# Attention loop of a bottleneck block on TensorE: in odd steps, maximum and logits ahead of the value product of four steps back

## What is computed

```python
qkv = conv2d(x, qkv_w, 0).reshape(b, 3, HEADS, HD, hw)
q, k, v = (qkv[:, 0], qkv[:, 1], qkv[:, 2])
r = (rw + rh).reshape(1, HEADS, HD, hw)
logits = jnp.einsum('bhdi,bhdj->bhij', q, k + r) * HD ** (-0.5)
a = jax.nn.softmax(logits, axis=-1)
out = jnp.einsum('bhij,bhdj->bhdi', a, v)
```

## Time and profile before

| | us |
|---|---|
| median of 3 runs | 3366.75 (3364.51 to 3368.51) |
| the profiled execution | 3367.39 |
| its span on the core | 3365.7 |
| PE busy | 3077.0 |
| DVE busy | 1934.3 |
| ACT busy | 1616.3 |
| POOL busy | 873.6 |

### The profile page before, as it was taken

How to read it: one execution, slowest core, us unless ns; L and a number is a source line. 1 busy time by engine, 2 the same in 40 slices (tenths; PEclk the granted TensorE clock), 3 DMA queues, 4 the chain that set the end, 5 groups by cost and what they waited for, 6 DMA issues and landing times.

```text
span 3365.7 us, 61219 instructions
## 1 busy us (share of the span) xinstructions
PE 3077.0 (91%) x27308; PEld 1574.1 (47%) x27308; DVE 1934.3 (57%) x2575; ACT 1616.3 (48%) x1870; POOL 873.6 (26%) x664
## 2 busy tenths in 40 slices
PE   3779989999999989999999899999899999998997
PEld 3534444454544545444444445445454454445453
DVE  5537565474755656465654757546564657537474
ACT  1315475172733646255651738326462456517382
POOL 1114141041411322132411414113231324014041
PEclk8889999999999999999999999999999999999998
DMA  4200000200011000100001000110001000000001
GB/s 143 73 26 29 1 29 26 78 2 29 11 49 46 2 29 20 57 29 1 30 26 66 14 29 8 38 60 2 29 20 57 29 1 30 26 29 27 1 8 44
DMA packets 35896, 105.61 MB, mean 31 GB/s; under 512 B 12976, under 2 KB 15024, under 8 KB 32944
## 3 DMA queue, kind: packets, MB, share of 16 engines
q1 hardware_dynamic: 35632, 101.69, 8.5%
HBM read 80.18 MB, written 21.50 MB: 30 GB/s over the span
## 4 chain that ended last, share of the span: by engine, by line
PE 70%; DVE 11%; ACT 7%; issue 7%; POOL 4%; DMA 1%; SPq 0%; POOLq 0%; DVEq 0%
PE ps_u L676 42%; PE ps_u L835 12%; DVE row_max L1192 4%; PE ps_o L857 3%; PE ps_o L858 3%; ACT wide L981 3%; PE ps_o L859 3%; PE ps_u L809 3%; ACT ps_u L981 2%; DVE probs L1202 1%; POOL wide L1300 1%; PE ps_u L695 1%; POOL y_pad L1300 1%; ACT probs L985 1%; DVE qk L1181 1%
## 5 line engine op out<-in xcount | busy, mean ns | idle before, releaser
L676 PE MATMUL ps_u<-y_pad,w_c 128*128 128x512 f16 x3456 | 789.5, 386 | 0.0
L1192 DVE TENSOR_REDUCE row_max<-ps_u 128x2 f32<-128x1024 f32 x512 | 619.8, 1221 | 219.6 <-PE ps_u L809 219.3
L1320 POOL TENSOR_TENSOR probs<-wide,probs 128x1024 f16<-128x1024 f32 x224 | 477.2, 2130 | 501.7 <-ACT probs L985 492.4
L676 PEld LDWEIGHTS ps_u<-y_pad,w_c 128*128 128x128 f16 x3456 | 331.3, 98 | 425.2 <-issue 24.2
L1002 DVE SCALAR_TENSOR_TENSOR wide<-wide 128x512 f32<-128x512 f32 x256 | 175.5, 688 | 608.9 <-ACT wide L903 606.7
L835 PE MATMUL ps_u<-qk 64*128 64x512 f16 x3072 | 425.2, 383 | 73.3 <-DVE probs L1202 24.9
L902 ACT ACTIVATE wide<-ps_u,par_m_t 128x512 f32<-128x512 f32 x128 | 99.3, 775 | 758.2 <-PE ps_u L676 758.2
L857 PEld LDWEIGHTS ps_o<-v_ext,probs 128*128 128x128 f16 x4096 | 375.7, 96 | 143.5 <-issue 129.0
L857 PE MATMUL ps_o<-v_ext,probs 128*128 128x65 f16 x4096 | 431.2, 193 | 0.0
L858 PE MATMUL ps_o<-v_ext,probs 128*128 128x64 f16 x4096 | 429.0, 195 | 0.0
L859 PE MATMUL ps_o<-v_ext,probs 128*128 128x65 f16 x4096 | 426.5, 191 | 0.0
(11 more groups left out here) (180 smaller groups left out, 3788.9 us busy)
## 6 DMA issues: line engine op xcount, KB each, us to landing
w_c<-w_c_dram SPq DMA_DIRECT2D x15, 2304.0 KB, 8.9
xn<-in_x_dram SPq DMA_DIRECT2D x32, 512.0 KB, 5.9
o_nat<-in_x_dram SPq DMA_DIRECT2D x64, 256.0 KB, 2.6
out_dram<-qk SPq DMA_DIRECT2D x32, 512.0 KB, 2.7
w_c_dram<-w_c SPq DMA_DIRECT2D x2, 2304.0 KB, 8.0
qk<-in_L_conv_m_cv_w_dram SPq DMA_DIRECT2D x2, 1152.0 KB, 6.9
probs<-in_L_conv_m_cv_w_dram SPq DMA_DIRECT2D x2, 1152.0 KB, 11.1
probs<-in_L_conv_cv_w_dram SPq DMA_DIRECT2D x2, 1024.0 KB, 11.8
```

The costliest lines, as they stand in the source:

```text
L676: ins = e.matmul(o, lhsT, rhs, start=start and k == 0, stop=stop and k == len(pairs) - 1)
L1192: e.reduce_max(row_max[:, g % 2, :, it, half], ps_u[:, use.slot:use.slot + 2, :], axis=AX.X).then_inc(*dve_max.up(i, b, g, half, it))
L1320: e.tensor_tensor(p_part(s, 1), wide[:, w.slot, :], p_part(s, 0), ALU.subtract).then_inc(*pool_lo.up("p", i, b, s))
```

## The change

```diff
--- before.py
+++ after.py
@@ -480,7 +480,7 @@
             late = None
             for s in range(STEPS):
-                if s >= LAG:
+                if s >= LAG and s % 2 == 0:
                     plan_av(s - LAG)
                 next(maxima, None)
                 if s in (1, 3):
@@ -498,6 +498,8 @@
                 late = None if w else (i, b, s, use)
                 if s in begins:
                     begins[s]()
+                if s >= LAG and s % 2:
+                    plan_av(s - LAG)
                 for thread in threads:
                     next(thread, None)
```

## The result

The changed kernel takes 3531.45 us (median of 4 runs, 3530.15 to 3533.23) against 3366.4 for the kernel before (median of 4): a ratio of 1.0489, 95% interval 1.0472 to 1.0505. It is slower by 165 us, where the prediction said 135, and its range ended at 3530. The profiled execution has a span of 3530.1 us against 3365.7, 164.4 more.

What follows compares the result with a forecast made beforehand. TensorE, busy for 91% of the span, was taken as the bound. Waits of 8.13 us a loop, times 16, gave 130 us; with 5 for the clock, 3367.4 became 3502, range 3445 to 3530.

Steps and rivals of the forecast that it cites:

- The three times 0.75: Pairs 4/5, 10/11, 16/17: odd logits, held by an exponential, start no earlier and the av comes behind; 2.25 us a loop.
- the 0.61 of the exponentials: Pair 14/15: also held by an exponential, but its odd logits had about 0.14 to spare; 0.61 us more a loop.
- the 0.53 of the shift row: Pair 6/7: L7 still waits for the shift row's copy and the av goes behind; 0.53 us more a loop.
- the 0.21s of the max: Pairs 8/9, 12/13, 18/19: odd logits wait for `row_max`; 0.21 us twice, 0.42 a loop, nothing at 12/13.
- `normalise` at steps 12, 20 and 28: Clearing of `ps_o` waits for `normalise`: 0.91 us at step 12, 2.25 at 20; 1.57 from step 24 to the end.
- the gain at step 21: Steps 20 to 24: L21 starts 0.94 us sooner, L22's exponential waits 0.53 longer; 0.41 us less a loop.
- the term of the clock: Half clock in newly opened holes of the loops: 5 us in all, between bounds of 0 and 34.
- the third hole of my count: The clock's upper bound counted three new holes of 1.3 to 2.3 us in each loop, each losing 0.7 us.
- five loops of 16: Sparse steps at a loop's head: half clock already costs five of 16 loops about 0.7 us before the change.
- The one on the clock: Rival: the clock falls in every hole, giving 3531 us or somewhat more; chance 0.09.
- The tiling rival: Rival: 14 fewer tiling changes a loop at 0.18 us each, without the waits, 40 us less, 3327; chance 0.04.
- Only the logits' waits: Rival: VectorE reaches `normalise` in time, so a loop keeps 3.40 us, 54 us in all, 3422; chance 0.07.

Runs made afterwards that it cites:

- the kernel with both holes filled: Changed kernel with the max of step 7 issued seven times and that of step 20 put ahead of the av and issued nine times: 3491.26 us.
- step 7 filled: Changed kernel with the two matmuls of the max of step 7 issued seven times in a row instead of once: 3507.75 us.
- step 7 as before: Changed kernel with step 7 alone in the earlier order, av ahead of max and logits: 3481.84 us.

## Why the prediction was off

**The waits.** The three times 0.75 and the 0.61 of the exponentials, the 0.53 of the shift row, the 0.21s of the max, `normalise` at steps 12, 20 and 28, the gain at step 21: the kernel with both holes filled has them within 0.1 us in a loop, in the sum and at each place of the table. Direction and mechanism were right. With the waits alone, and the av behind L31 that adds 0.65 to each loop's tail (0.75 in the layout), the change costs 16 x (7.27 + 0.65) = 127 us, for 130 forecast; 7.27 is the filled kernel's 7.06 and the max of 0.22 that it moves away, and the clean loops with step 7 filled say 7.26.

**The step that failed** is the term of the clock: "I take 5", in a range of 0 to 34. In the trace it is 27 falls in new holes: 16 at step 7 at 1.5 us and 11 at step 20 at 1.3 to 1.4 us, 25 + 15 = 40 us in the loops; one more head at half clock adds 0.3, and the joins gave 3 back. 127 + 40 - 3 and 1 us ahead of the first loop make 165, for the 164.4 of the spans. Both factors of my bound were off. The price of 0.7 was read where half clock fell on sparse steps, with logits that wait anyway (0.21 in the earlier trace rows); behind the new holes it falls on two avs or on av and logits that nothing hides (3.38 us for 2.12 from L7's last pair to L8). And the share was argued from a hole of 1.22 us that never had a fall; the new ones are 1.88 and 2.08 us. At steps 12 and 28, with 1.12 and 1.04, the clock did not fall, so the third hole of my count was none. Why a hole of 2.08 us has a fall in 11, 7 or none of 16 loops, by kernel, stays open. The prediction's "five loops of 16" that lose 0.7 at their head are six in the trace, which changes nothing in its sum.

**The rivals.** The one on the clock, with 0.09, named 3531, which is what was measured. The kind of cause was right and the figure in part luck: two holes and a price of some 1.5, and one of them not in every loop, instead of three and 0.7. The range ended 1 us below it, and 0.09 was too little: a bound that is worked out from a price in a place with slack is no upper bound. The tiling rival is out by its own rule (idle time under 0.18 us in a pair): in the pairs with a max the least idle time ahead of the odd logits was 0.24, where the clock was full, and a change saved is worth about 0.2. "Only the logits' waits" is out by the clearing's 67.9 us of waits.

## What to carry to other kernels

A piece with no wait of its own, placed between two dependent ones, is worth its whole length as cover; moving it costs exactly that when the dependent piece can't start sooner, and each pair has to be asked for its holder. When a change opens a hole on TensorE, the idle time is only the first part of the price: the dense work behind it may run at half clock, so it is to be priced at the density of what follows. A small gain that the trace shows and the time does not is worth a second look once the holes elsewhere are filled.

## What the runs showed of the hardware

Twelve matmuls in each loop that compute nothing new made the kernel 24 us faster: behind them the granted clock stayed at 1.00 in all 16 loops, where half clock had followed in all 16. Holes of 1.88 us at step 7 were followed by half clock in 16 of 16 loops of the changed kernel, and holes of 1.04 to 1.22 us at steps 7, 12, 20 and 28 in none. A hole of 2.08 us at step 20 was followed by half clock in 11 of 16 loops of the changed kernel, in 7 with step 7 filled, and in none with step 7 as before. What in the timing decides is open, and only one execution of each kernel has a trace; the times of four executions lie within 3.1 us in the changed kernel and within 5.5 with step 7 filled. A change from 128-row to 64-row matmuls and back cost about 0.2 us a time in the steps where nothing waits, and nothing where the logits wait anyway.
